# Weight parts and edge rows repeated four times in two bytes, in a graph kernel's table stage

## The reference, cut to what matters

```python
scores = jnp.einsum('ehd,ehd->eh', q[src], k[dst])
smax = jax.ops.segment_max(scores, src, num_segments=N)
ex = jnp.exp(scores - smax[src])
denom = jax.ops.segment_sum(ex, src, num_segments=N)
out = jax.ops.segment_sum((ex / denom[src])[:, :, None] * v[dst], src, num_segments=N)
...
msgs = x[col] * vals[:, None]                       # vals = edge_weight
agg = jax.ops.segment_sum(msgs, row, num_segments=n)
```

## Time and profile before

| what | value |
|---|---|
| median of 3 runs | 1852.47 us |
| profiled execution | 1853.64 us |
| its span | 1851.8 us |
| PE busy (share of the span) | 1741.4 us (94%) |
| DVE busy | 1252.2 us (68%) |
| ACT busy | 857.5 us (46%) |
| POOL busy | 399.2 us (22%) |
| mean granted TensorE clock | 0.988 |

### The profile page before, as it was taken

The page is one execution under the profiler, slowest core; times in us unless marked ns, Lnnn a source line. Parts: engine busy times, 40 slices in busy tenths (PEclk is TensorE's granted clock), DMA queues, the critical chain, the costliest instruction groups (busy, mean ns, idle before and its releaser), DMA issues.

```text
span 1851.8 us, 28469 instructions
## 1 busy us (share of the span) xinstructions
PE 1741.4 (94%) x10800; PEld 1469.5 (79%) x10800; DVE 1252.2 (68%) x2234; ACT 857.5 (46%) x1539; POOL 399.2 (22%) x500
## 2 busy tenths in 40 slices
PE   4666999999999999999999999999999999999998
PEld 3444778888887888888888888887888888878777
DVE  8999865675856557658665666677557657675844
ACT  7665454454542445445434454455335446453221
POOL 1002130010381301001743010005621001036201
PEclk9998999999999999999999999999999999999899
DMA  3042452232310324224202332332104224241121
GB/s 126 1 130 86 193 161 89 95 129 89 118 35 23 105 77 141 95 79 135 62 23 64 104 128 85 100 117 74 40 25 134 88 78 150 83 145 37 42 91 63
DMA packets 63876, 168.48 MB, mean 91 GB/s; under 512 B 5957, under 2 KB 24250, under 8 KB 63735
## 3 DMA queue, kind: packets, MB, share of 16 engines
q10 hardware_dynamic: 23040, 102.41, 17.0%
q1 hardware_dynamic: 40700, 64.25, 10.9%
HBM read 145.04 MB, written 16.99 MB: 88 GB/s over the span
## 4 chain that ended last, share of the span: by engine, by line
PE 76%; DVE 11%; issue 6%; ACT 3%; POOL 2%; DMA 1%; DVEq 1%; ACTq 0%; POOLq 0%; SPq 0%
PE ps L1476 65%; PE ps L1692 9%; DVE prob L1229 2%; PE ps L1610 2%; DVE CW L1076 2%; DVE left L1037 1%; DVE PT_lo L1245 1%; DVE left L1043 1%; ACT prob L828 1%; POOL x L636 1%; ACT PT_hi L846 1%; DMA piece<-in_L_gnn_m_w_dram 1%; PE ps L1910 1%; ACT right L776 0%; DVE k_lo L1208 0%
## 5 line engine op out<-in xcount | busy, mean ns | idle before, releaser
L846 ACT ACTIVATE PT_hi<-ps 128x512 fp32r<-128x512 f32 (+1 forms) x400 | 235.5, 589 | 244.6 <-PE ps L1692 244.4
L1245 DVE TENSOR_TENSOR PT_lo<-ps,PT_hi 128x512 fp32r<-128x512 f32 (+1 forms) x400 | 270.1, 676 | 51.2 <-ACT PT_hi L846 43.7
L828 ACT ACTIVATE prob<-prob,nmax 128x1250 f32<-128x1250 f32 x160 | 214.1, 1338 | 137.4 <-DVE nmax L1229 137.4
L1692 PE MATMUL ps<-ident,prob 128*128 128x128 f32 (+1 forms) x1600 | 245.3, 276 | 12.7 <-DVE PT_lo L1245 11.6
L1229 DVE CUSTOM_DVE_ANT_0 prob<-ps,Lr 128x1250 f32<-128x1250 f32 x160 | 232.3, 1452 | 31.9 <-PE ps L1476 30.6
L1692 PEld LDWEIGHTS ps<-ident,prob 128*128 128x128 f32 (+1 forms) x1600 | 179.5, 140 | 80.4 <-DVE PT_lo L1245 61.7
L1476 PE MATMUL ps<-PT_hi,v_hi 128*128 128x256 f32 (+1 forms) x800 | 226.7, 283 | 1.2 <-DVE PT_lo L1245 1.2
L1476 PE MATMUL ps<-PT_lo,v_hi 128*128 128x256 f32 (+1 forms) x800 | 225.0, 281 | 0.0
L1476 PE MATMUL ps<-PT_hi,v_lo 128*128 128x256 f32 (+1 forms) x800 | 224.4, 280 | 0.0
L1476 PE MATMUL ps<-yT,wqk_hi 128*128 128x512 f32 (+1 forms) x768 | 213.1, 364 | 0.0
L1476 PE MATMUL ps<-k_hi,q_hi 128*128 128x512 f32 (+2 forms) x480 | 191.5, 399 | 2.1 <-DVE k_lo L1208 2.1
(11 more groups left out here) (210 smaller groups left out, 3600.3 us busy)
## 6 DMA issues: line engine op xcount, KB each, us to landing
Lr<-l_table ACTq DMA_DIRECT2D x160, 625.0 KB, 3.9
piece<-in_L_gnn_m_w_dram SPq DMA_DIRECT2D x32, 256.0 KB, 2.8
w_table<-CW SPq DMA_DIRECT2D x5, 1250.0 KB, 7.4
prob<-w_table SPq DMA_DIRECT2D x10, 625.0 KB, 4.0
x<-in_x_dram SPq DMA_DIRECT2D x2, 2304.0 KB
CW<-CW SPq DMA_DIRECT2D x7, 625.0 KB
piece<-in_L_gnn_wo_dram SPq DMA_DIRECT2D x16, 256.0 KB, 4.9
piece<-in_L_gnn_wq_dram SPq DMA_DIRECT2D x15, 256.0 KB, 2.8
```

What stands on the lines that cost most here:

```text
L828: act.activation(buf, buf, ACT.Exp, bias=nmax[:, i % 4:i % 4 + 1], scale=-1.0, accum_out=prob[:, i % 3, N:N + 1]).then_inc(S["exped"], 1)
L846: act.activation(o, i, ACT.Copy).then_inc(S["pt_hi"], 1)
L1245: dve.tensor_tensor(lo, i, hi.bitcast(F32), ALU.subtract).then_inc(S["pt_split"], 1)
L1692: m = pe.transpose(bank(5 + n % 2, at * P, at * P + rows), prob[0:rows, (NT * h + 2 * g + j) % 3, d * P:(d + 1) * P], ident[0:rows, 0:rows])
```

## The change

- wpart gets the shape [P, NG, 3, GK, 4]: each part of each weight stands four times side by side. The three casts that fill it (L1019, L1023, L1025) write 672 elements each in place of 168.
- A new tile row16 [P, NG, GK, 4] in f16 (two bytes) holds each edge's row number four times. It is filled straight from PSUM in the place of the copy to eT[:, 4].
- rows(n) compares iota_h with row16 and weigh(n) multiplies with wpart, both seen as 32 repeats (step zero) of a run of 4 (step one), so that the innermost step of every operand is one. The number of elements stays 384 and 1152.
- left is laid out [P, SBUFS, 4, GK, P], parts outside and blocks inside, so that weigh writes and reads one run. TensorE's index into left is changed to suit; its matmuls are the same.

```diff
-            left = sb("left", [P, SBUFS, GK, 4, P], BF16, prep)
+            left = sb("left", [P, SBUFS, 4, GK, P], BF16, prep)
...
-            wpart = sb("wpart", [P, 3, NG, GK], BF16, prep)
...
+            wpart = sb("wpart", [P, NG, 3, GK, RUN], BF16, prep)
+            row16 = sb("row16", [P, NG, GK, RUN], F16, prep)
...
-            parts = [wpart[:, i].rearrange("p g b -> p b g") for i in range(3)]
-            link(dve.tensor_copy(parts[0], weight))
+            def runs(table):
+                return table.rearrange("p g b r -> p b g r")
+
+            def repeated(values):
+                return values.unsqueeze(3).to_broadcast([P, GK, NG, RUN])
+
+            parts = [runs(wpart[:, :, i]) for i in range(3)]
+            link(dve.tensor_copy(parts[0], repeated(weight)))
             dve.wait_ge(edges_turned, 2)
-            turned(4, 0)
-            link(dve.tensor_tensor(wres[:], weight, parts[0], ALU.subtract))
-            link(dve.tensor_copy(parts[1], wres[:]))
-            link(dve.tensor_tensor(wres[:], wres[:], parts[1], ALU.subtract))
-            link(dve.tensor_copy(parts[2], wres[:]))
+            dve.tensor_copy(runs(row16), repeated(bank(0, 0, cols).rearrange("p (b g) -> p b g", b=GK)))
+            link(dve.tensor_tensor(wres[:], weight, parts[0][:, :, :, 0], ALU.subtract))
+            link(dve.tensor_copy(parts[1], repeated(wres[:])))
+            link(dve.tensor_tensor(wres[:], wres[:], parts[1][:, :, :, 0], ALU.subtract))
+            link(dve.tensor_copy(parts[2], repeated(wres[:])))
...
+            def over(run):
+                return run.unsqueeze(2).to_broadcast([P, run.shape[1], P // RUN, RUN])
+
             def rows(n):
-                dve.tensor_tensor(left[:, n % SBUFS, :, 0, :], iota_h[:, 0:P].unsqueeze(1).to_broadcast([P, GK, P]),
-                                  eT[:, 4, :, n].unsqueeze(2).to_broadcast([P, GK, P]), ALU.is_equal).then_inc(e_onehot, 1)
+                dve.tensor_tensor(left[:, n % SBUFS, 0].rearrange("p b (m r) -> p b m r", r=RUN),
+                                  iota_h[:, 0:P].rearrange("p (m r) -> p m r", r=RUN).unsqueeze(1).to_broadcast([P, GK, P // RUN, RUN]),
+                                  over(row16[:, n]), ALU.is_equal).then_inc(e_onehot, 1)
 
             def weigh(n):
                 dve.wait_ge(e_onehot, n + 1)
-                factors = left[:, n % SBUFS]
-                dve.tensor_tensor(factors[:, :, 1:4, :], factors[:, :, 0, :].unsqueeze(2).to_broadcast([P, GK, 3, P]),
-                                  wpart[:, :, n, :].rearrange("p k b -> p b k").unsqueeze(3).to_broadcast([P, GK, 3, P]),
-                                  ALU.mult).then_inc(e_parts, 1)
+                dve.tensor_tensor(left[:, n % SBUFS, 1:4].rearrange("p k b (m r) -> p (k b) m r", r=RUN),
+                                  left[:, n % SBUFS, 0].rearrange("p b c -> p (b c)").unsqueeze(1).to_broadcast([P, 3, GK * P]),
+                                  over(wpart[:, n].rearrange("p k b r -> p (k b) r")), ALU.mult).then_inc(e_parts, 1)
```

More of the change, by code:

```diff
@@ L48 @@
 SBUFS = 4
+RUN = 4
 AHEAD = SBUFS - 1
@@ L261, in build @@
             wres = sb("wres", [P, GK, NG], F32, prep)
-            wpart = sb("wpart", [P, 3, NG, GK], BF16, prep)
             right = sb("right", [P, SBUFS, GK, PLACES], F8, prep)
-            after_right = sb("after_right", [P, 248], F32, prep)
-            after_y1 = sb("after_y1", [P, 24], F32, prep)
+            after_right = sb("after_right", [P, 528], F32, prep)
             iota_h = sb("iota_h", [P, NP], F16, prep)
@@ L1134, in _ @@
                                 m = dve.tensor_tensor(oh_dst[:, 1 + part, :], oh_dst[:, 0, :],
-                                                      wpart[:, part, bass.ds(g, 1), b].to_broadcast([P, N]), ALU.mult)
+                                                      wpart[:, bass.ds(g, 1), part, b, 0:1].rearrange("p o r -> p (o r)").to_broadcast([P, N]), ALU.mult)
                             m.then_inc(g_onehot, 1)
@@ L1554, in _ @@
                             o = ps[:, at:at + PLACES] if part == 0 else ps[:, at + 512:at + 512 + PLACES]
-                            m = mm(o, left[:, n % SBUFS, b, part, :], right[:, n % SBUFS, b, :],
+                            m = mm(o, left[:, n % SBUFS, part, b, :], right[:, n % SBUFS, b, :],
                                    b == 0 and part < 2, b == GK - 1 and part in (0, 3))
```

## The result

The changed kernel takes 1825.64 us (median of 4 runs, 1824.48 to 1826.23); the kernel before, beside it, 1852.74. The ratio is 0.985, 95% interval 0.9836 to 0.9863: 27.1 us less. Forecast were 1822 us and a gain of 30.6. In the profiled execution the span is 1824.4 us, 27.4 less, and tables_done comes 27.7 us earlier: the gain is in the table stage, and what stands behind it took the same time to 0.3 us. Code lines are 1 to 11 higher after the change; weigh is L1054, rows L1048, the addition L1087, value_load L1083.

The account below looks back on a forecast made before the run. VectorE, without idle, was taken to bound the table stage. Gains by stretch, less 1.75 us of preparation, sum to 30.6 us: 1853.6 to 1823.0 profiled, 1822 us as median; range 1814 to 1836.

Parts of the forecast that it names:

- The halving: VectorE's weigh and rows run at two elements a cycle, 0.60 and 0.20 us less a group.
- one of the two, or neither, doubles: Rivals on weigh and rows: weigh alone 1827 us, rows alone 1846, 8% together; no change in rate 1854, 5%.
- short runs are read slowly: Rival on weigh and rows: two-byte short pieces read at 1.67 cycles an element, 1914 us; 4%.
- The loop of 3.23 us for two groups: Steady groups: addition, matmuls and handovers between VectorE and TensorE allow 1.62 us a group, a gain of 0.765.
- a slower handover: Rival, matmuls' end to addition: the 0.75 us grows behind a shorter queue, steady group 1.8 us, 1828 us; 12%.
- The preparation: Before group 0: three casts and one copy write 672 elements in place of 168, 1.75 us later.
- bound of 0.61 us for a faster cast: Preparation: casts take 0.61 us each if they go faster, the low end of its 0.8 to 3.6 us cost.
- "+0" at two places: From the sine to addition 15 and at additions 22 to 24: waits take the gain, so +0 each.
- rival of ten slow groups: TensorE's clock stays at the lower level for ten more groups, 12 us lost, 1834 us; 6%.
- turn_cond: TensorE at group 35: 0.7 us of work has 0.2 of idle to hide in, no longer 0.79; costs 0.5 us.
- the first groups: Additions 1 to 4, held back by TensorE's slow first matmuls: 6.95 us in place of 9.6, gain 2.65.
- x: Its load, needed for the statistics behind addition 51, follows row stores 10.6 us earlier; 10 us of cover.

Follow-up runs that it names:

- e1: Changed kernel with rows reading the two-byte row16 with a step of zero again, weigh as changed; 1827.5 us.
- e3: Changed kernel with weigh reading wpart with a step of zero in the new layout, rows as changed; 1849.7 us.
- e2: Changed kernel with row16 four-byte (f32), still runs of four with step one; 1831.75 us, a single run.
- e4: Changed kernel with runs of two in place of four; 1824.05 us.
- e6: Changed kernel with value_load put ahead of the wait for TensorE's group; 1821.65 us.
- e12: Changed kernel with runs of two, make_cond spread over groups 18 to 27, ten filling matmuls ahead of third hidden_cond, next group's value_load right behind each addition; 1810.69 us.
- e8: Changed kernel with ten matmuls of 512 columns, result unread, on TensorE ahead of the third hidden_cond; 1823.9 us.
- e9: Changed kernel with make_cond cut into ten node tiles, one ahead of each of TensorE's groups 18 to 27; 1821.7 us.
- e11: e10 with fourteen matmuls of 512 columns, result unread, on TensorE behind the fourth hidden_cond; 1820.7 us.
- e10: e9 with the third and fourth hidden_cond ahead of TensorE's group 17 in place of 15; 1828.4 us.

## Why the prediction was right, and where a size was off

1. The bound (VectorE, by its lack of idle time) and the place of the gain (ahead of tables_done, nothing behind it) were right.
2. The halving was right for both operations: 0.748 and 0.348 us by the sum, 751 and 351 ns measured. The rivals that one of the two, or neither, doubles, and that short runs are read slowly, fell with these lengths; e1 to e3 show which condition does it. By the rule that the prediction cites from the Trainium skill (Vector Engine (DVE) Microarchitecture Reference, 5.1 Performance modes — why throughput varies by op and dtype) the altered operation of e1, e2 and e3 had to be at the single rate, and it was (548, 549 and 1348 ns); that the run may be as short as two is e4's.
3. The loop of 3.23 us for two groups gave 1.62 us; measured is 1.623. e6 and e12, which take the register load out of it, have 1.586. The rival of a slower handover fell (its price counts 31 groups where its own list has 33: 5.9 us and not 5.6).
4. The preparation: casts of 0.85 us were right, but -1.75 was met by luck. The two subtractions that read wpart between them grew from 0.33 to 0.46 us, which I had not charged, and VectorE's last operation before the groups comes 2.03 us later. ScalarE's table load, ahead of its first right, comes only 1.70 later, and so does addition 0; why it follows 0.33 us closer is open. First before, then after:
```profile
14.62 0.14 DVE L1032 TENSOR_SCALAR grow_i<-viol 1x1 int32<-1x1 f32 x1
16.27 1.28 ACT L776 ACT_TABLE_LOAD   x1 [1.65 <-issue]
```
```profile
16.65 0.14 DVE L1040 TENSOR_SCALAR grow_i<-viol 1x1 int32<-1x1 f32 x1
17.97 1.28 ACT L777 ACT_TABLE_LOAD   x1 [3.43 <-issue]
```
   The prediction's bound of 0.61 us for a faster cast follows from no row: half of the elements' time and the fixed part would be 0.50.
5. The step that was mis-sized is "+0" at two places, from the sine to addition 15 and from 21 to 24. The waits there took the gain, as I had said, but they also grew, by 1.3 and 1.5 us, 2.8 of the 2.9 us by which tables_done missed the sum. I had the clock only as a rival of ten slow groups with 6%, priced 12 us, and none of it in the forecast, though at both places before had a slow spell of 3.4 us already. At the first, e8 and the traces without a spell show the cause: 12.8 us without one, which is 1.1 less than before, and 15.2 with one of 6.8 us. (Nor did ScalarE work there without a gap, as the prediction says: before, it waited 0.87 us for TensorE's last two hidden_cond, and after, 1.73.) At make_cond the clock is seen in the windows, and the length follows the spell: 9.8 us in e6 with one of 3.4, 11.75 in the changed kernel with 6.8, 12.8 in e4 with 10.2. e9, which removes the block, has none. No run changes the clock there and nothing else, so at make_cond the cause is argued.
6. turn_cond cost 0.9 us and not 0.5, and the first groups gave 0.35 more than I had; between them they nearly cancel. The first groups vary by more than that: additions 1 to 4 took 6.6 us in the changed kernel and up to 7.5 in e11, with the same work.
7. x: its load was issued at 114.78 us, 7.1 earlier and not 10.6, since the row parts' stores came only 8.2 earlier and their issues took 11.69 us in place of 10.98. The transfers faded by 126 us, and addition 51 was at 135: still covered.

## What to carry to other kernels

Before you halve an engine's work, write down the next loop with all its links, the register load among them: here it was 0.03 us a group behind VectorE, and taking the load out of it gave 1.9 us in the steady stretch and more at the places where VectorE waits for TensorE. A gain in front of a wait for another engine is lost, and where that engine is TensorE, its clock can cost more than the wait: an idle of 3.5 us in e10 was followed by 20 us at half clock, and filling it in e11 gave 7.7 us. Look at the granted clock at each such place before, and give it a term in the sum. And repeat a per-partition factor only as often as is needed to make the innermost step one: twice was as good as four times.

## What the runs showed of the hardware

- VectorE's two operations with two tensors took 0.52 ns an element in place of 1.04 when every operand was two-byte and its innermost run had a step of one (351 and 751 ns), also where that run was two elements long and was repeated by a step of zero outside it (e4: 350 and 750 ns).
- The slow clock can outlast its cause: in e10 it fell in 3.5 us of idle and then stayed at 0.50 for 19 us more, with TensorE busy in all of them. In the other traces the spells between 30 and 130 us lasted 3.4, 6.8 or 10.2 us.
- Much the same idle ahead of hidden_cond (2.2 to 2.4 us) was followed by a slow spell in the changed kernel, e2, e3 and e6, and by none in e1, e4 and e9. And at make_cond the clock fell 3.4 us after that block's start in the changed kernel (from 78.9), while before it fell only when the block was done (from 87.15 to 91.7). What decides this is open, and with one trace of each kernel it is not known whether a kernel's own runs differ in it. Before addition 15 a spell is worth up to 2.4 us (15.2 against 12.8).
